# Two of three head groups transposed in 32x32 squares by VectorE and by way of DRAM, in a newly ordered attention pipeline

## Chip, cores and metric

The kernel runs on one core of a Trainium2 chip. The metric is the device time of one execution in microseconds (us); lower is better. All data is fp32.

## What is computed

Thirty-two batches of 256 rows of 384 numbers go through one attention layer with 12 heads of 32 columns. A per-batch matrix `adj` (256 x 256) is added to the scores of every head. Then comes the residual and a layer norm:

```
q = (x @ Wq.T).reshape(B, N, 12, 32)
k = (x @ Wk.T).reshape(B, N, 12, 32)
v = (x @ Wv.T + bv).reshape(B, N, 12, 32)
a = einsum('bnhd,bmhd->bhnm', q, k) * 384**-0.5 + adj[:, None]
a = where(all(a == 0, axis=-1), -inf, a)
a = nan_to_num(softmax(a, axis=-1))
o = einsum('bhnm,bmhd->bnhd', a, v).reshape(B, N, 384)
y = layernorm(x + o @ Wo.T + bo)
```

## The kernel before

The five engines are programmed by hand, each in its own block, and meet through semaphores. Each engine runs a function `step(t)` over the batches (a few steps written out, a loop of two steps per turn, a few more written out). Within an engine the order of the work is the order in which `step` calls its helpers, and nothing else decides it. In step t the kernel *attends* batch t, *finishes* batch t-1 and *projects* batch t+1.

Per batch, the work is this (P = 128 partitions, N = 256 rows in two halves, 12 heads in three groups of four):

- **Projection** (`unit`, helper `product`, L487). K and Q come as three units K01, K2Q0, Q12, V as V0, V1. Each fp32 product is made of three passes over pieces split in high and low parts. ScalarE copies K and Q out of PSUM (`save_kq`, L382), GpSimd splits them (`split_kq`, L292, L294), VectorE adds the bias to V (`save_v`, L746). GpSimd also splits the next x (`split_xt`, L279, L281).
- **Scores** (`scores`, L564), one group at a time, into the four `s_bank`s. VectorE adds `adj`, negates and finds the row's least value in one instruction per head and half (`add_bias`, L724). ScalarE takes the exponential and the row sum (`exps`, L395) into `prob`, a ring of four units. A *unit* is two heads of one half; a batch has 12, units 0 to 3 being group 0, and so on.
- **Transposing**. For the product with V the keys must lie on the partitions. TensorE transposes every unit of `prob` with four matmuls by the identity (`transposes`, L578) into one of two `t_bank`s. VectorE (units 0, 2, 4, 6, 8, 10, L736) and ScalarE (the odd ones, L406) copy the result into `probT`.
- **Weighing** (`weigh`, L615): `probT` times V, 8 matmul pairs per group, into `bank_a`. ScalarE copies it out (`save_o`, L414).
- **Finish**: the reciprocal of the sums (L784) is widened by GpSimd (L312), transposed by TensorE (`spread`, L592), multiplied in (`divide`, L793). ScalarE and GpSimd split the result (L422, L303), TensorE multiplies it by Wo (Y0, Y1), VectorE adds the residual (L803) and takes the moments (L808, L813), GpSimd makes the deviation (`deviation`, L321 to L326), ScalarE normalises (L428). A small matmul (`flag`, L623) looks for rows that are all zero.

The DMAs are all issued by SyncE's queue, in order: per step xt (the transposed x, 384 KB), bias (`adj`, 256 KB), xr (x, 384 KB) and the store of the output (384 KB). PSUM has eight banks: four `s_bank`s, two `t_bank`s, `bank_a` (weighing, spread, K01, flag) and `bank_b` (everything else). In TensorE's step the order is

```
T10 T11 | K2Q0 | weigh 2 | T0 T1 | Q12 | spread | scores 1 | T2 T3 | spread | V0 | weigh 0 | T4 T5
V1 | scores 2 | T6 T7 | K01 | Y0 | T8 T9 | weigh 1 | scores 0 of the next | flag | Y1
```

where T10, T11, weigh 2, spread, Y0 and Y1 belong to batch t-1 and K, Q, V to batch t+1.

Of the kernel before, what the change touches and what calls it, by code (L numbers as in the profile page):

```python
# [3 lines left out]
F32 = mybir.dt.float32  # L4
# [9 lines left out]
P = 128  # L14
# [4 lines left out]
UNITS = H * NT // PAIR  # L19
SCALE = D ** -0.5  # L20
# [5 lines left out]
PT_RING = 2 * JH  # L26
# [4 lines left out]
ON_DVE = (0, 2, 4, 6, 8, 10)  # L31


class Unit:


    def __init__(self, u):
        self.u, self.g, self.c, self.pair = u, u // 4, u // 2 % 2, u % 2
        self.heads = [JH * self.g + PAIR * self.pair + i for i in range(PAIR)]


class Step:


    def __init__(self, i, c):
        self.i, self.c, self.n, self.p = i, c, 2 * i + c, c % 2
        looped = not isinstance(i, int)
        self.attend = looped or 0 <= c < B
        self.finish = looped or 1 <= c <= B
        self.project = looped or -1 <= c <= B - 2  # L50
        self.looped = looped
        self.first = not looped and c == 0
        self.last = not looped and c == B

    def count(self, per_step, extra=0):
        return self.i * (2 * per_step) + (self.c * per_step + extra)

    def before(self):
        return Step(self.i, self.c - 1)

    def after(self):
        return Step(self.i, self.c + 1)

    def slot(self, h):
        return (JH * self.p + h) % PT_RING

    def kq(self, name):

        order = ("K01", "K2Q0", "Q12") if not self.looped and self.c == -1 else ("K2Q0", "Q12", "K01")
        return self.count(3, 3 + order.index(name) + 1)  # L70

    def copies(self, u, on_dve):

        mine = [k for k in range(UNITS) if (k in ON_DVE) == on_dve]
        return self.count(len(mine), len([k for k in mine if k <= u]))

    def unit(self, u):
        return (self, u) if u >= 0 else (self.before(), u + UNITS)


def steps(eng, body):
    for c in range(-1, 3):
        body(Step(0, c))
    with eng.Fori(1, (B - 4) // 2) as i:
        body(Step(i, 1))
        body(Step(i, 2))
    for c in range(B - 3, B + 2):
        body(Step(0, c))


def build(nc, x, xT, adj, wqT, wkT, wvT, bv, woT, bo, out):
# [15 lines left out]
    bias = [sb(f"bias{p}", [P, NT, N]) for p in range(2)]  # L107
    kq = sb("kq", [P, 2 * KC, N])
# [7 lines left out]
    probT = sb("probT", [P, PT_RING, NT, N])  # L116
# [21 lines left out]
    t_bank = [nc.alloc_psum_tensor(f"t_bank{k}", [P, PAIR, NT, P], F32) for k in range(2)]  # L138

    bank_a = nc.alloc_psum_tensor("bank_a", [P, NT * N], F32)  # L140

    bank_b = nc.alloc_psum_tensor("bank_b", [P, NT * N], F32)
# [13 lines left out]
    bias_loaded = [sem(f"bias_loaded{p}") for p in range(2)]  # L156
    xt_hi_ready = sem("xt_hi_ready")
    xt_ready = sem("xt_ready")
    xr_ready = sem("xr_ready")
    kq_done = sem("kq_done")  # L160
    kq_saved = sem("kq_saved")
    kq_hi_ready = sem("kq_hi_ready")
    kq_ready = sem("kq_ready")
# [10 lines left out]
    pv_done = sem("pv_done")  # L174
    o_saved = sem("o_saved")
# [22 lines left out]
    def on_a(t, name):  # L198
        if not t.looped and t.c == -1:
            return name in ("K01", "Q12", "V1")  # L200
        return name == "K01"

    def bank(t, name):
        return bank_a if on_a(t, name) else bank_b

# [3 lines left out]
    with nc.Block() as block:  # L209

        @block.sync
        def _(sp):
            def load_xt(t, k):
                sp.dma_start(xt[(t.c + k) % 2][:], xT[t.n + k].rearrange("(c p) n -> p c n", p=P)
                             ).then_inc(xt_loaded[(t.c + k) % 2], DMA)

            def load_bias(t):
                q = (t.c + 1) % 2
                sp.dma_start(bias[q][:], adj[t.n + 1].rearrange("(c p) m -> p c m", p=P)
                             ).then_inc(bias_loaded[q], DMA)  # L220
# [7 lines left out]
            load_xt(Step(0, 0), 0)  # L228
# [3 lines left out]
            load_bias(Step(0, -1))  # L232
            load_xt(Step(0, 0), 1)
            load_w(W_V, wvT)
            load_b(bv_all, bv)
            load_b(bo_all, bo)
            load_w(W_O, woT)

            def step(t):
                if t.c == -1:  # L240
                    sp.wait_ge(xt_ready, 1)
                    load_xt(t, 3)
                if t.looped or 0 <= t.c <= B - 4:

                    sp.wait_ge(xt_ready, t.count(1, 2))
                    load_xt(t, 3)
                if t.project and (t.looped or t.c >= 0):
                    if t.looped or t.c >= 1:

                        sp.wait_ge(neg_ready, t.count(H * NT))  # L250
                    load_bias(t)
                if t.attend:
                    if t.looped or t.c >= 2:

                        sp.wait_ge(y_saved, t.count(NT, -NT))
                    sp.dma_start(xr[t.p][:], x[t.n].rearrange("(c p) d -> p c d", p=P)
                                 ).then_inc(xr_loaded[t.p], DMA)
                if t.before().finish:
                    sp.wait_ge(y_ready, t.count(NT, -NT))
                    sp.dma_start(out[t.n - 2].rearrange("(c p) d -> p c d", p=P), y_out[:]  # L260
                                 ).then_inc(stored, DMA)
# [5 lines left out]
        def _(pool):  # L267
# [7 lines left out]
            def split_xt(t, k):  # L275
                q = (t.c + k) % 2
                pool.wait_ge(xt_loaded[q], DMA * ((t.c + k) // 2 + 1) + t.i * DMA)
                apart(pool)
                nc.gpsimd.tensor_copy(xt_hi[q][:], xt[q][:]).then_inc(xt_hi_ready, 1)  # L279
                pool.wait_ge(xt_hi_ready, t.count(1, k + 1))  # L280
                nc.gpsimd.tensor_tensor(xt_lo[q][:], xt[q][:], xt_hi[q][:].bitcast(F32), ALU.subtract  # L281
                                        ).then_inc(xt_ready, 1)

            def split_kq(t, name):
                q = (t.c + 1) % 2
                a = KQ_AT[name]
                if t.looped or t.c >= 1:

                    pool.wait_ge(scored, t.count(KC))
                pool.wait_ge(kq_saved, t.kq(name))  # L290
                apart(pool)
                nc.gpsimd.tensor_copy(kq_hi[q][:, a:a + 2, :], kq[:, a:a + 2, :]).then_inc(kq_hi_ready, 1)  # L292
                pool.wait_ge(kq_hi_ready, t.kq(name))
                nc.gpsimd.tensor_tensor(kq_lo[q][:, a:a + 2, :], kq[:, a:a + 2, :],  # L294
                                        kq_hi[q][:, a:a + 2, :].bitcast(F32), ALU.subtract).then_inc(kq_ready, 1)

            def split_o_lo(t):
                if t.looped or t.c >= 2:

                    pool.wait_ge(y_done, t.count(NT, -NT))  # L300
                for k, (a, b) in enumerate(((0, 2), (2, 3))):
                    pool.wait_ge(o_hi_ready, t.count(2, k - 1))
                    nc.gpsimd.tensor_tensor(o_lo[:, a:b], o_n[:, a:b], o_hi[:, a:b].bitcast(F32), ALU.subtract  # L303
                                            ).then_inc(o_ready, 1)

            def widen_inv(t):
                pool.wait_ge(inv_ready, t.count(1))
                if t.looped or t.c >= 2:

                    pool.wait_ge(inv_spread, t.count(2, -2))  # L310
# [4 lines left out]
            def deviation(t):  # L315

                pool.wait_ge(stats_ready, t.count(NT))
                if t.looped or t.c >= 2:
                    pool.wait_ge(y_ready, t.count(NT, -NT))
# [3 lines left out]
                pool.wait_ge(var_ready, t.count(2))  # L323
                nc.gpsimd.tensor_tensor(rstd[:], var_eps[:], halfs[:], ALU.pow).then_inc(pow_ready, 1)
                pool.wait_ge(pow_ready, t.count(1))
                nc.gpsimd.tensor_tensor(shift[:], negmean[:], rstd[:], ALU.mult).then_inc(rstd_ready, 1)  # L326

            def add_bo(t):
                pool.wait_ge(b_loaded, 2 * DMA)
                pool.wait_ge(xr_loaded[t.p], DMA * (t.c // 2 + 1) + t.i * DMA)  # L330
# [3 lines left out]
            def step(t):  # L334
                if t.c == -1:
                    for name in ("K01", "K2Q0", "Q12"):
                        split_kq(t, name)
                    pool.wait_ge(xt_ready, 1)
                    split_xt(t, 2)
                    return  # L340
                if t.finish:
                    widen_inv(t)
                if t.project:
                    split_kq(t, "K2Q0")
                if t.before().finish:
                    deviation(t.before())
                if t.project:
                    split_kq(t, "Q12")
                if t.finish:
                    split_o_lo(t)  # L350
                if t.looped or 0 <= t.c <= B - 3:

                    pool.wait_ge(kq_done, t.count(3, 3))
                    pool.wait_ge(v_done, t.count(2, 2))
                    split_xt(t, 2)
# [543 lines left out]
```

## Time and profile before

| | |
|---|---|
| time, median of 3 runs | 851.68 us (850.9 to 851.9) |
| time of the profiled execution | 852.93 us |
| its span, first to last instruction | 850.9 us |
| TensorE (PE) busy | 826.5 us, 97% |
| ScalarE (ACT) busy | 645.2 us, 76% |
| VectorE (DVE) busy | 557.8 us, 66% |
| GpSimd (POOL) busy | 454.6 us, 53% |
| moved by DMA | 49.30 MB, mean 58 GB/s |
| mean granted TensorE clock | 0.986 |

The profiled execution took 1.25 us more than the median of the runs. Its span leaves out 2.0 us of its own time, which lie before the first and after the last instruction. Matmuls and weight loads are pipelined, so a matmul's own duration is longer than the time it adds. What a group of matmuls costs is read from the chain of waits, which gives each piece of the chain its start, its length and the number of instructions in it.

### The profile page before, as it was taken

How to read it: one execution, taken by the hardware profiler on the slowest of the kernel's cores; microseconds unless marked ns; L12 is line 12 of the kernel's file. 1: busy time of each engine (PE TensorE's matmuls, PEld its weight loads, DVE VectorE, ACT ScalarE, POOL GpSimd, SP SyncE). 2: the span in 40 equal slices, each digit the busy share in tenths (PEclk: the TensorE clock that was granted, in tenths of full speed). 3: DMA queues.
4: the chain of work that ended last, by engine and by line, in shares of the span. 5: the costliest groups of instructions: out<-in, count | busy, mean ns of one | idle time of the engine just before them, and what ended most of it. 6: DMA issues, size and time to landing. Idle time of an engine off the chain costs nothing.

```text
span 850.9 us, 27334 instructions
## 1 busy us (share of the span) xinstructions
PE 826.5 (97%) x8504; PEld 715.3 (84%) x8504; DVE 557.8 (66%) x2152; ACT 645.2 (76%) x2055; POOL 454.6 (53%) x518
## 2 busy tenths in 40 slices
PE   7999999999999999999999999999999999999974
PEld 6888888888888888888888888888888888888853
DVE  3666676766666676667676667676667676667672
ACT  3677787877787877777877777887777787777782
POOL 4455545655545655545655545665454665454522
PEclk8999999999999999999999999999999999999996
DMA  6211221211221111222111222111222110211010
GB/s 198 70 44 40 70 70 52 66 39 47 68 68 55 62 47 39 68 68 66 51 53 33 68 68 68 49 55 31 68 68 68 49 61 25 68 50 51 21 39 37
DMA packets 40864, 49.30 MB, mean 58 GB/s; under 512 B 2176, under 2 KB 40832, under 8 KB 40832
## 3 DMA queue, kind: packets, MB, share of 16 engines
q1 hardware_dynamic: 40832, 48.90, 18.6%
q8 instruction: 17, 0.28, 0.1%
q14 instruction: 15, 0.12, 0.1%
HBM read 36.31 MB, written 12.58 MB: 57 GB/s over the span
## 4 chain that ended last, share of the span: by engine, by line
PE 95%; ACT 1%; DVE 1%; issue 1%; POOL 1%; DMA 1%; SPq 0%; ACTq 0%; POOLq 0%; DVEq 0%
PE bank_b L487 41%; PE t_bank L578 21%; PE bank_a L615 11%; PE s_bank L564 10%; PE bank_a L487 8%; PE bank_a L592 2%; ACT prob L395 1%; DMA w_f<-in_wkT 1%; DVE neg L724 0%; PE bank_a L623 0%; POOL o_lo L303 0%; ACT y_out L428 0%; DVE probT L736 0%; POOL kq_lo L294 0%; DVE y L803 0%
## 5 line engine op out<-in xcount | busy, mean ns | idle before, releaser
L395 ACT ACTIVATE prob<-neg,negmax 128x256 f32<-128x256 f32 x768 | 379.8, 499 | 2.9 <-DVE negmax L724 2.8
L724 DVE CUSTOM_DVE_ANT_0 neg<-s_bank,bias 128x256 f32<-128x256 f32 x768 | 281.0, 419 | 39.0 <-PE s_bank L564 37.7
L578 PE MATMUL t_bank<-ident,prob 128*128 128x128 f32 x1536 | 207.4, 278 | 2.8 <-ACT prob L395 2.8
L578 PEld LDWEIGHTS t_bank<-ident,prob 128*128 128x128 f32 x1536 | 169.0, 140 | 41.3 <-ACT prob L395 18.6
L406 ACT ACTIVATE probT<-t_bank 128x512 f32<-128x512 f32 x192 | 113.4, 591 | 105.5 <-PE t_bank L578 105.5
L312 POOL COPY inv_wide<-inv 128x768 f32<-128x768 f32 x32 | 26.4, 824 | 250.3 <-DVE inv L784 250.3
L395 ACT ACTIVATION_READ_ACCUMULATOR prob<-neg,negmax 128x1 f32 x768 | 146.9, 191 | 0.0
L736 DVE COPY probT<-t_bank 128x512 f32<-128x512 f32 x192 | 131.6, 685 | 1.3 <-PE t_bank L578 1.2
L294 POOL TENSOR_TENSOR kq_lo<-kq,kq_hi 128x512 fp32r<-128x512 f32 x96 | 123.6, 1287 | 7.7
L487 PE MATMUL bank_b<-xt_hi,w_hi 128*128 128x256 f32 x378 | 112.7, 298 | 0.0
L487 PE MATMUL bank_b<-xt_lo,w_hi 128*128 128x256 f32 x378 | 107.0, 283 | 0.0
L487 PE MATMUL bank_b<-xt_hi,w_lo 128*128 128x256 f32 x378 | 107.0, 283 | 0.0
L292 POOL CAST kq_hi<-kq 128x512 fp32r<-128x512 f32 x96 | 58.7, 612 | 87.9 <-ACT kq L382 76.8
L615 PE MATMUL bank_a<-probT,v 128*32 128x256 f32 x1536 | 102.8, 385 | 2.6 <-DVE probT L736 1.8
L803 DVE TENSOR_TENSOR y<-bank_b,xr 128x384 f32<-128x384 f32 x64 | 35.7, 557 | 80.0 <-PE bank_b L487 80.0
L793 DVE TENSOR_TENSOR o_n<-o_raw,bank_a 128x512 f32<-128x512 f32 x64 | 35.1, 549 | 69.1 <-PE bank_a L592 69.1
L303 POOL TENSOR_TENSOR o_lo<-o_n,o_hi 128x512 fp32r<-128x512 f32 x64 | 64.8, 1013 | 23.6 <-ACT o_hi L422 23.6
L487 PEld LDWEIGHTS bank_b<-xt_hi,w_hi 128*128 128x128 f32 x378 | 72.5, 192 | 3.6 <-issue 2.4
L487 PEld LDWEIGHTS bank_b<-xt_lo,w_hi 128*128 128x128 f32 x378 | 72.7, 192 | 0.0
L487 PEld LDWEIGHTS bank_b<-xt_hi,w_lo 128*128 128x128 f32 x378 | 72.4, 192 | 0.0
L487 PE MATMUL bank_b<-w_hi,o_hi 128*128 128x384 f32 x192 | 69.1, 360 | 3.1 <-POOL o_lo L303 2.5
L615 PEld LDWEIGHTS bank_a<-probT,v 128*32 128x32 f32 x1536 | 40.3, 109 | 36.8 <-issue 12.9
(70 smaller groups left out, 1738.6 us busy)
## 6 DMA issues: line engine op xcount, KB each, us to landing
xt<-in_xT SPq DMA_DIRECT2D x32, 384.0 KB, 3.5
xr<-in_x SPq DMA_DIRECT2D x32, 384.0 KB, 3.1
out_y<-y_out SPq DMA_DIRECT2D x32, 384.0 KB, 2.5
bias<-in_adj SPq DMA_DIRECT2D x32, 256.0 KB, 2.7
w_f<-in_wkT SPq DMA_DIRECT2D x3, 192.0 KB, 4.0
w_f<-in_wqT SPq DMA_DIRECT2D x1, 576.0 KB, 6.0
w_f<-in_wvT SPq DMA_DIRECT2D x1, 576.0 KB, 7.8
w_f<-in_woT SPq DMA_DIRECT2D x1, 576.0 KB, 10.2
```

What stands on the lines that cost most here:

```text
L292: nc.gpsimd.tensor_copy(kq_hi[q][:, a:a + 2, :], kq[:, a:a + 2, :]).then_inc(kq_hi_ready, 1)
L294: nc.gpsimd.tensor_tensor(kq_lo[q][:, a:a + 2, :], kq[:, a:a + 2, :], kq_hi[q][:, a:a + 2, :].bitcast(F32), ALU.subtract).then_inc(kq_read ...
L303: nc.gpsimd.tensor_tensor(o_lo[:, a:b], o_n[:, a:b], o_hi[:, a:b].bitcast(F32), ALU.subtract).then_inc(o_ready, 1)
L395: nc.scalar.activation(prob[:, u % PROB_RING, k], neg[:, h, w.c], ACT.Exp, scale=-1.0, bias=negmax[t.p][:, w.c, h:h + 1], accum_out=sums[t ...
L406: nc.scalar.activation(probT[:, a:a + PAIR, :, P * w.c:P * (w.c + 1)], t_bank[u % 2][:], ACT.Copy).then_inc(probT_act, 1)
L487: last = nc.tensor.matmul(ps, w_pair[a](k), m_pair[b](k), start=(k == 0 and e == 0), stop=(k == KC - 1 and e == 2))
L564: last = nc.tensor.matmul(s_bank[j][:, c, :], a[t.p][rows, KC + g, P * c:P * (c + 1)], b[t.p][rows, g, :], start=(e == 0), stop=(e == 2))
L578: last = nc.tensor.transpose(t_bank[u % 2][:, k, m, :], prob[:, u % PROB_RING, k, P * m:P * (m + 1)], ident[:])
L615: last = nc.tensor.matmul(bank_a[HD * j:HD * (j + 1), 0:N], v[t.p][:, m, HD * h:HD * (h + 1)], probT[:, t.slot(h), m, :], start=(m == 0), ...
L724: nc.vector.tensor_tensor_reduce(out=neg[:, h, w.c], in0=s_bank[h % JH][:, w.c, :], in1=bias[t.p][:, w.c, :], scale=-1.0, scalar=BIG, op0= ...
L736: nc.vector.tensor_copy(probT[:, a:a + PAIR, :, P * w.c:P * (w.c + 1)], t_bank[u % 2][:]).then_inc(probT_dve, 1)
L803: nc.vector.tensor_tensor(y[:, c, :], bank(t, f"Y{c}")[:, 0:D], xr[p][:, c, :], ALU.add).then_inc(y_saved, 1)
```

## The change

**Groups 0 and 1 are no longer transposed by TensorE.** For units 0 to 7, VectorE transposes `prob` in squares of 32 x 32 (`square`, new L794 to L805), one instruction per unit, from SBUF to a staging area in SBUF. That area lies over `w_f`, the raw weights, which are no longer needed after their split. The squares then still lie on the wrong partitions. So SyncE stores each group (128 partitions x 8 KB, 1 MB) to a buffer in DRAM and loads it back in another order of rows (`store_squares`, `load_squares`, new L247 to L262), with runs of 2 KB. `weigh` reads the loaded tile in runs of 32 elements. ON_DVE is empty: the copies of the four units that TensorE still transposes (8 to 11) are all ScalarE's.

**Keys in a row.** For the load to have whole runs, keys 4r+b of a half are put in place 32b+r: `save_kq` writes K01 in that order, and groups 0 and 1 take `adj` from a second copy, `adjP`, with its columns in the same order (made once on the host, outside the device's time). This adds one DMA of 256 KB per step (`bias_sq`). Group 2 reads the first `adj` against scores whose K2 lies in the old order.

**Banks.** The two `t_bank`s become one (`bank_t`), and the bank so freed is `bank_c` (K01 and spread). `bank_a` keeps the weighing and the flag, `bank_b` the rest.

**Orders and stages.** The order of every engine is new. In step t, TensorE attends batch t from its scores 2 on, projects K01 and V0 of batch t+1 and makes its scores 0 and 1, projects K2Q0 and Q12 of batch t+2, weighs groups 1 and 2 of batch t-1 and multiplies batch t-2 by Wo. There are separate semaphores for the three K and Q units and for the three groups of the weighing.

```diff
-PT_RING = 2 * JH
-ON_DVE = (0, 2, 4, 6, 8, 10)
+SQ = 32
+BLOCKS = P // SQ
+SQUARED = 2
+TURNED = SQUARED * GROUP
+ON_PE = tuple(range(TURNED, UNITS))
+ON_DVE = ()
...
+    bias_sq = [sb(f"bias_sq{p}", [P, NT, N]) for p in range(2)]
+    probT = sb("probT", [P, H - SQUARED * JH, NT, N])
+    sq_probT = [sb(f"sq_probT{g}", [P, BLOCKS, JH, NT, NT, SQ]) for g in range(SQUARED)]
+    AREA = BLOCKS * JH * NT * NT * SQ
+    w_space = w_f[:].rearrange("p w c n -> p (w c n)")
+    sq_dram = [nc.dram_tensor(f"sq_dram{g}", (P, BLOCKS, AREA // BLOCKS), F32, kind="Internal").ap()
+               for g in range(SQUARED)]
...
-    t_bank = [nc.alloc_psum_tensor(f"t_bank{k}", [P, PAIR, NT, P], F32) for k in range(2)]
+    bank_t = nc.alloc_psum_tensor("bank_t", [P, PAIR, NT, P], F32)
...
+            def store_squares(t, g):
+                sp.wait_ge(squared, t.count(TURNED, GROUP * (g + 1)))
+                after(sp, sq_loaded[g], t.count(DMA))
+                sp.dma_start(sq_dram[g], sq_stage[g].rearrange("p b h m c s -> p b (h m c s)")
+                             ).then_inc(sq_stored[g], DMA)
+            def load_squares(t, g):
+                sp.wait_ge(sq_stored[g], t.count(DMA, DMA))
+                after(sp, pv_done[g], t.count(1))
+                sp.dma_start(sq_probT[g][:].rearrange("p i h m c s -> p i (h m c s)"),
+                             sq_dram[g].rearrange("(i r) b n -> (r b) i n", i=BLOCKS)).then_inc(sq_loaded[g], DMA)
...
 # SyncE's step
+                if t.alive:
+                    store_squares(t, 0)
+                    load_squares(t, 0)
+                    store_squares(t, 1)
+                    load_xr(t)
+                    load_squares(t, 1)
+                if nxt2.alive and not nxt2.first:
+                    load_bias_sq(nxt2)
+                if prev2.alive:
+                    store_out(prev2)
...
+            def square(t, u):
+                w = Unit(u)
+                dve.wait_ge(prob_ready, t.count(H * NT, PAIR * (u + 1)))
+                if u % GROUP == 0:
+                    after(dve, sq_stored[w.g], t.count(DMA))
+                a = w.heads[0] % JH
+                nc.vector.transpose(sq_stage[w.g][:, :, a:a + PAIR, :, w.c].rearrange("p b h m s -> p (h m) b s"),
+                                    prob[:, u % PROB_RING].rearrange("p k (m b r) -> p (k m) b r", m=NT, b=BLOCKS)
+                                    ).then_inc(squared, 1)
...
 # TensorE's weigh
+                if g < SQUARED:
+                    pe.wait_ge(sq_loaded[g], t.count(DMA, DMA))
...
+                        if g < SQUARED:
+                            weights = sq_probT[g][:, :, j, m].rearrange("p i c s -> p c i s")
+                        else:
+                            weights = probT[:, h - SQUARED * JH, m, :]
```

TensorE's new order of a step (names as above; -1 and -2 are the batches before, +1 and +2 those after):

```
T11(-1) | V1 | K01(+1) | Y0(-2) | weigh 1(-1) | scores 2 | K2Q0(+2) | weigh 2(-1) | T8 | Y1(-2)
spread(-1) | flag | T9 | scores 0(+1) | Q12(+2) | weigh 0 | T10 | spread(-1) | V0(+1) | scores 1(+1)
```

How instructions move, at three places. First TensorE in the middle of a step. Before, between Q12 (`bank_b`) and V0, two units of transposes stand back to back (eight matmuls) behind the scores (`s_bank`):

```order
L592 MATMUL bank_a<-ident,inv_wide 128x128 x4
L564 MATMUL s_bank<-kq_hi 128x256 x4
L564 MATMUL s_bank<-kq_lo,kq_hi 128x256 x4
L564 MATMUL s_bank<-kq_hi,kq_lo 128x256 x4
L564 MATMUL s_bank<-kq_hi 128x256 x4
L564 MATMUL s_bank<-kq_lo,kq_hi 128x256 x4
L564 MATMUL s_bank<-kq_hi,kq_lo 128x256 x4
L578 MATMUL t_bank<-ident,prob 128x128 x8
```

Now, from the last product of Q12 on, with `sq_probT` the tile that came back from DRAM:

```order
L539 MATMUL bank_b<-xt_hi,w_lo 128x256
L626 MATMUL bank_a<-sq_probT,v 32x256 x8
L596 MATMUL bank_t<-ident,prob 128x128 x4
L607 MATMUL bank_c<-ident,inv_wide 128x128 x2
L539 MATMUL bank_b<-w_hi,xt_hi 128x384
```

Only single units of four transposes are left, and each stands between other work.

Second, VectorE. Before, between `add_bias` of units 9 and 10 (each head an instruction and its read of the accumulator), a copy out of PSUM:

```order
L724 ISA neg,negmax<-s_bank,bias 128x256
L724 ISA negmax 128x1
L736 COPY probT<-t_bank 128x4x128
L724 ISA neg,negmax<-s_bank,bias 128x256
L724 ISA negmax 128x1
```

Now, behind unit 3's `add_bias` at the beginning of a step (`w_f` is the staging area):

```order
L789 ISA neg,negmax<-s_bank,bias_sq 128x256
L789 ISA negmax 128x1
L803 STREAM_TRANSPOSE w_f<-prob 128x4x4x32
L823 TENSOR_TENSOR v<-bank_b,bv_all 128x384
L803 STREAM_TRANSPOSE w_f<-prob 128x4x4x32
```

Six copies a step are gone and eight square transposes are in.

Third, SyncE's queue with its waits. Before, a step:

```order
L214 DMA xt<-in_xT 128x3x256 [waits xt_ready]
L219 DMA bias<-in_adj 128x2x256 [waits neg_ready]
L256 DMA xr<-in_x 128x2x384 [waits y_saved]
L260 DMA out_y<-y_out 128x2x384 [waits y_ready]
```

Now a step, from the second half of the loop:

```order
L252 DMA sq_dram<-w_f 128x2048 [waits squared,sq_loaded0]
L256 REGISTER_ALU
L261 DMA sq_probT<-sq_dram 128x4x512 [waits sq_stored0,pv_done0]
L248 REGISTER_ALU
L252 DMA sq_dram<-w_f 128x2048 [waits squared,sq_loaded1]
L245 ISA [waits y_saved]
L245 DMA xr<-in_x 128x2x384
L261 DMA sq_probT<-sq_dram 128x4x512 [waits sq_stored1,pv_done1]
```

Four DMAs of 1 MB per step are new, and each load waits in the queue for its own store to have landed.

## Rows read from the trace of the kernel before

**Rows 1.** The profile's page, section 1: busy time of each engine over the span

```profile
PE 826.5 (97%) x8504; PEld 715.3 (84%) x8504; DVE 557.8 (66%) x2152; ACT 645.2 (76%) x2055; POOL 454.6 (53%) x518
```

**Rows 2.** Busy by stretch, two whole steps inside the loop

```profile
core 0: us, PE busy (x) PEld busy (x) DVE busy (x) ACT busy (x) POOL busy (x), PEclk, DMA share, GB/s
300.11:350.92 50.81, 50.81 (x531) 44.15 (x531) 34.36 (x135) 39.91 (x128) 28.44 (x32) 1.00 0.18 57
```

**Rows 3.** Chain of waits inside the loop: start us, us, what

```profile
299.24 0.87 PE t_bank L578 x8
...
304.49 2.16 PE bank_b L487 x18
306.65 0.44 PE bank_a L592 x4
307.08 0.91 PE s_bank L564 x24
308.00 1.02 PE t_bank L578 x8
309.02 0.22 PE bank_a L592 x2
309.24 1.59 PE bank_b L487 x9
310.83 1.00 PE bank_a L615 x16
...
322.88 0.12 PE bank_a L623
```

**Rows 4.** The same chain, where steps 1, 2 and 30 begin

```profile
45.20 1.11 PE t_bank L578 x8
...
70.68 0.87 PE t_bank L578 x8
...
781.86 0.87 PE t_bank L578 x8
```

**Rows 5.** VectorE's timeline: start us, us, line, tiles, shapes, count

```profile
300.53 0.69 DVE L736 COPY probT<-t_bank 128x512 f32<-128x512 f32 x1
301.13 0.41 DVE L724 CUSTOM_DVE_ANT_0 neg<-s_bank,bias 128x256 f32<-128x256 f32 x1
301.47 0.42 DVE L724 CUSTOM_DVE_ANT_0 neg<-s_bank,bias 128x256 f32<-128x256 f32 x1
```

**Rows 6.** Groups by form: count, busy us, mean ns of one, idle before

```profile
L395 ACT ACTIVATE prob<-neg,negmax 128x256 f32<-128x256 f32 x768 | 379.8, 499 | 2.9 <-DVE negmax L724 2.8
L406 ACT ACTIVATE probT<-t_bank 128x512 f32<-128x512 f32 x192 | 113.4, 591 | 105.5 <-PE t_bank L578 105.5
L281 POOL TENSOR_TENSOR xt_lo<-xt,xt_hi 128x768 fp32r<-128x768 f32 x31 | 57.4, 1851 | 2.5
```

**Rows 7.** DMA issues: KB each, median us from issue to landing

```profile
xr<-in_x SPq DMA_DIRECT2D x32, 384.0 KB, 3.1
out_y<-y_out SPq DMA_DIRECT2D x32, 384.0 KB, 2.5
bias<-in_adj SPq DMA_DIRECT2D x32, 256.0 KB, 2.7
```

**Rows 8.** Busy by stretch while the first loads run

```profile
4.00:10.00 6.00, 4.69 (x26) 3.71 (x25) 3.13 (x6) 2.73 (x4) 0.00 (x0) 0.86 1.01 335
8.00:14.00 6.00, 5.78 (x35) 5.78 (x36) 1.53 (x2) 2.15 (x3) 1.90 (x2) 0.72 1.05 300
```

**Rows 9.** Chain of waits, the end of the last batch

```profile
824.43 0.66 PE t_bank L578 x4
...
836.22 3.23 PE bank_b L487 x9
...
840.09 3.26 PE bank_b L487 x9
```

More of the change, by code:

```diff
@@ L61, in after, with count @@
[L61 to L70, printed above, removed]
+        self.looped = not isinstance(i, int)
+        self.alive = self.looped or 0 <= c < B
+        self.first = not self.looped and c == 0
+    def count(self, per_batch, extra=0):
+        return self.i * (2 * per_batch) + (self.c * per_batch + extra)
@@ L239, in step @@
             def step(t):
[L240 to L261, printed above, removed]
+                nxt2 = t.later(2)
+                nxt = t.later(1)
+                prev2 = t.later(-2)
+                if nxt2.alive and (nxt2.looped or nxt2.c >= 2):
+                    load_xt(nxt2)
+                if nxt.alive and not nxt.first:
+                    load_bias(nxt)
+                if t.alive:
[8 more added lines that the diff above has]
+                    store_out(prev2)
             steps(sp, step)
@@ L334, in step @@
             def step(t):
[L335 to L355, printed above, removed]
-                if t.attend:
+                nxt2 = t.later(2)
+                nxt = t.later(1)
+                prev = t.later(-1)
+                prev2 = t.later(-2)
+                if prev.alive:
+                    widen_inv(prev)
+                if nxt2.alive and not nxt2.first:
+                    split_xt(nxt2)
+                if nxt.alive:
+                    split_kq(nxt, "K2Q0")
+                    split_kq(nxt, "Q12")
+                    split_kq(nxt, "K01")
+                if prev2.alive:
+                    deviation(prev2)
+                if t.alive:
                     add_bo(t)
-                if t.project:
-                    split_kq(t, "K01")
+                if prev.alive:
+                    split_o_lo(prev, 0)
+                    split_o_lo(prev, 1)
             steps(pool, step)
@@ L635, in step @@
             def step(t):
-                if t.c == -1:
-                    for name in ("K01", "K2Q0", "Q12"):
-                        unit(t, name)
-                    scores(t.after(), 0)
-                    return
-                if t.first:
-                    unit(t.before(), "V0")
-                    unit(t.before(), "V1")
-                if t.finish:
-                    transposes(t.before(), 10)
-                    transposes(t.before(), 11)
-                if t.project:
-                    unit(t, "K2Q0")
```

717 lines of the change are left out of this document (368 added, 349 removed).

## Prediction

> **What bounds the kernel now.** I read the page's busy shares first [rows 1]: TensorE is busy for 97% of the span, ScalarE for 76, VectorE for 66. Such shares are means over stages, so I took the busy table of two steps inside the loop next [rows 2]: there TensorE is busy for 50.81 of 50.81 us at the full granted clock (1.00, the 2.4 GHz level), ScalarE for 39.91, VectorE for 34.36, GpSimd for 28.44, and the DMA engines for 0.18 of the time. So a step takes 25.4 us and TensorE alone sets it. The chain of waits says the same: in the loop it holds TensorE pieces only, and these lengths are what each piece adds [rows 3]. A K or Q unit costs 2.16, a V or Y unit 1.59, a weighing 1.00, scores of a group 0.91, the two spreads 0.44 and 0.22, the flag 0.12, and two units of transposes 0.87 or 1.02. Six such pairs stand in a step, two at 0.87 and four at 1.02, 5.8 us together. Check: 3 x 2.16 + 4 x 1.59 + 3.0 + 2.73 + 0.66 + 0.12 + 5.8 = 25.2, the 25.4 of the table but for 0.2. Steps begin at 45.20 (step 1), 70.68 (step 2) and 781.86 (step 30) [rows 4]: 28 steps in 711.2 us. The rest of the 850.9 us is 70.7 of head and 69.0 of tail.
>
> **TensorE.** Eight of twelve units leave. The four left stand alone between other work. A pair costs 0.15 more behind weighing or scores than behind a projection (1.02 against 0.87), so a unit alone is not half a pair: its lower end is 0.51, its upper one the 0.66 of a lone unit in the tail [rows 9]. I take 0.55, nearer the loop's row, since the tail's unit had just waited: 2.2 us a step in place of 5.8. The step becomes 25.4 - 3.6 = 21.8 us. The weighings of groups 0 and 1 read their tile in runs of 32; no row shows such a read. I keep 1.00 each, because the tile is as large and the runs are long, with 1.5 as upper end (1 us a step).
>
> **VectorE.** Two steps hold 34.36 us of its work, 17.2 in one. Six copies go. A copy of 512 elements starts 0.60 before the next instruction (300.53 to 301.13) [rows 5], so 13.6 us stay. What a square transpose of 512 elements takes is not in this trace. Lower end: half the elements' time; 256 elements in `add_bias` cost 0.34 from start to start [rows 5], 0.26 less than 512, so 0.34. Upper end: two ticks per element, 0.60 + 2 x 0.26 = 1.12. I take 0.60, the row with the same number of elements. 13.6 + 8 x 0.60 = 18.4 of 21.8 us. The Trainium skill, Vector Engine (DVE) Microarchitecture Reference, section on the reshape front-end, has the transposing array sustain one element per cycle and lane, which would be my 0.60; no run so far shows it.
>
> **ScalarE.** 19.96 us a step, less two copies of 0.59 at most [rows 6] and 0.5 in fact, since such durations overlap: 19.0 of 21.8. K01's copy now writes with a stride; at double its cost it adds 0.6, and 2 us of cover are left. Its 24 exponentials (499 ns and the accumulator's read) are untouched.
>
> **The DMAs.** A step moves 1.44 MB now (three times 384 KB and 256 KB). Added are 4 x 1.05 MB and 0.26: 5.9 MB. The rate: 57 GB/s at a share of 0.18 [rows 2] is 317 GB/s for a full share, and in the first loads full rings moved 335 and 300 [rows 8]. So 18.6 us of transfers a step (17.6 to 19.7): busy, but under 21.8. The round trip: 128 KB more cost 0.4 us (256 KB in 2.7, 384 in 3.1) [rows 7]; by that rate and the 317, a load of 1 MB takes 3.1 + 2.1 = 5.2 us and a store, from the 2.5 of the output's, 4.6.
>
> **Do the waits fit?** I laid one step along TensorE's new order, with 0 at T11. V1 ends at 2.1, K01 at 4.3, Y0 5.9, weigh 1 at 6.9, scores 2 at 7.8, K2Q0 at 10.0, weigh 2 at 11.0, Y1 13.1, scores 0 of the next 15.2, Q12 17.3, weigh 0 18.3, V0 20.7, scores 1 21.7. VectorE has unit 3's square (the fourth) behind it at 4.4: store at 9.0, load landed at 14.2, weigh 0 wants it at 17.3. 3 us to spare. Unit 7's square ends near 9.8. Its store queues behind that load, lands at 17.3, and the load goes out then: landed near 23.5, which is 1.7 of the next step, wanted at 5.9. 4 us to spare. The tightest places are others: scores 1 needs VectorE's unit 3 (0.5 us to spare); the second spread needs the first `divide` (0.8); K2Q0 of t+2 needs its x loaded and split. That x is issued behind the output's store, which waits in SyncE's queue for ScalarE's last `normalise` at 20.2. It then queues in the rings behind the 1 MB load, lands near 4 of the next step, takes 2.8 in GpSimd (1.85 of it the subtraction [rows 6]) and is wanted at 7.8, 1 us to spare. GpSimd's widening and splits fill the time up to 12.5, scores 0 wants them at 14.3. So no wait ends last in my table. Misses of 0.1 to 0.3 in single rows are covered, of 1 us not: 0 to 1 us of stall a step is the range, 0 my value.
>
> **Ends.** Head: the first Q unit has to wait for its weights as before, steps 0 and 1 miss parts. By the same table scores 1 of batch 0 end near 26 us; step 0 is ScalarE's (16), step 1 TensorE's without Y (21.8 - 3.2): 61 where the kernel before has 70.7. Tail: step 30 lacks two projections, and ScalarE then bounds it (18); from step 31 on I count 45 (T11, Y0, the last weighings, Y1, and then the last batch's finish with its two Y units at 3.2 each at the lower clock [rows 9]): 63 against 69.
>
> **Sum.** 61 + 28 x 21.8 + 63 = 734 us of span, plus the 2.0 outside it: **736 us**, against 852.9 of the profiled execution. The median of the runs was 1.25 lower than that execution; I leave this out.
>
> **Rivals.**
> 1. *VectorE becomes the bound.* A square takes 1.12 us: 13.6 + 9.0 = 22.6, and in its order it waits about 1 us more for Y0 and for scores: 23.6 a step, 736 + 28 x 1.8 = 786 us. For it: no row prices the square. Against it: the copy's row, with as many elements. Chance 0.13.
> 2. *The rings become the bound.* They idle where SyncE waits for a store to land before it issues the load, about 1.7 us for group 0 and 0.5 for group 1. With 5.9 MB the step is 5.9 MB / rate + 2.2: 20.8 us at 317 GB/s, 23.3 at 280. That gives 736 + 28 x 1.5 = 778 us. For it: half of the new bytes are written to DRAM at once before they are read, and 300 was the rate of one full stretch [rows 8]. Against it: longer runs (2 KB) than any in this trace. The Trainium skill, DMA: Bandwidth & Descriptors, section on latency, gives HBM access as 0.2 us on average and 2 us at high load. No row here shows the latter. An estimate by that page: each transfer takes 1.8 longer, the two gaps grow by 3.6, the step is 24.4 and the whole 809 us. Chance of this rival 0.17.
> 3. *Slower than before: the round trip through DRAM at a low rate.* The same loop of store, wait and load in SyncE's queue decides from 250 GB/s down: 23.6 + 2.2 = 25.8 a step, and 736 + 28 x 4.0 = 848. At 235 GB/s it is 27.3, 890 us. For it: stores and loads of 1 MB to and from one DRAM buffer are new. Against it: the 317 of the loop and the quick landing of the output's store. Chance 0.07.
>
> That the edit does not do what it says I rule out: the instruction order shows 4 of 12 units left on TensorE.
>
> **Numbers.** Forecast 0.62, its own range 722 to 757 (a unit of transposes at 0.51; 0.7 us of stall). The rest, 0.01, is a result near no change. A measurement of this kernel can tell 0.2% from none. The range must reach into rivals 1 and 2 and hold four fifths: 720 to 795. Faster 0.91, same 0.01, slower 0.08.
>
> **What would show it.** Steps of 21.8 us in the loop's busy table, with TensorE at over 20.8 of them. Square transposes near 0.60 from start to start. Landing of the 1 MB load near 5.2 and of the store near 4.6, a DMA share near 0.85. If the chain of waits holds VectorE's squares, rival 1 is right; if weigh 0 or the x split wait for a DMA, rival 2 or 3. A granted clock under 1.00 in the loop would mean stalls I left out, and a weighing piece over 1.00 for groups 0 and 1 a cost I set to nothing.

## Result, and the profile after

The changed kernel takes 881.47 us (median of 4 runs, 879.22 to 883.38), the kernel before 851.75 (850.9 to 851.9). The ratio is 1.035, with a 95% interval of 1.032 to 1.038. The forecast was 736.0 us, its range 720 to 795. The kernel is slower, and by none of the three rivals.

The page of the profile after: busy times, the granted clock and the DMA share in 40 slices, the queues, the chain by engine, some groups and the DMA issues (KB each, us to landing).

```profile
PE 748.5 (85%) x7480; PEld 636.9 (72%) x7480; DVE 597.4 (68%) x2216; ACT 618.7 (70%) x1991; POOL 452.1 (51%) x518
...
PEclk8989999899798988979899797998979989899965
DMA  7277787577374774747667375774747747477740
...
q14 instruction: 76, 0.62, 0.2%
...
PE 75%; issue 12%; DMA 4%; DVE 3%; POOL 2%; ACT 2%; SPq 0%; DVEq 0%; ACTq 0%; POOLq 0%
...
L803 DVE STREAM_TRANSPOSE w_f<-prob 128x512 f32<-128x512 f32 x256 | 173.1, 695 | 2.9 <-issue 2.8
...
sq_dram<-w_f SPq DMA_DIRECT2D x64, 1024.0 KB, 5.5
sq_probT<-sq_dram SPq DMA_DIRECT2D x64, 1024.0 KB, 5.7
```

The same two rows of the page before, which have no notches and few packets:

```profile
PEclk8999999999999999999999999999999999999996
...
q14 instruction: 15, 0.12, 0.1%
```

Against the page before [rows 1], TensorE's busy time fell from 826.5 to 748.5 us, as it was meant to, but its share fell from 97% to 85%: it waits. The granted clock is notched, which it was not before, and so is the DMA share. The chain holds 12% of "issue", time in which an engine waits for nothing that the profile shows.

Busy by stretch in the changed kernel: the second row runs free, the first and the third take in a notch (the columns are those of [rows 2]).

```profile
327.50:355.00 27.50, 24.57 (x241) 21.30 (x245) 19.65 (x75) 17.88 (x58) 12.16 (x14) 0.85 0.48 171
450.00:480.00 30.00, 30.00 (x324) 25.61 (x326) 24.33 (x97) 25.24 (x84) 17.46 (x20) 1.00 0.79 280
500.00:554.00 54.00, 46.53 (x467) 40.12 (x466) 36.82 (x138) 38.32 (x124) 28.60 (x33) 0.91 0.62 222
```

Between notches the kernel does what the prediction said: TensorE is busy for all of 30.00 us at clock 1.00 (the 2.4 GHz level), with the rings at a share of 0.79. The chain of waits shows what a notch is (start us, length us, what):

```profile
428.85 0.23 PE bank_c L607 x2
...
429.31 0.06 DVEq L85
429.36 5.11 issue
...
434.84 0.42 DVE neg L789
435.27 0.34 DVE neg L789
435.61 2.29 issue
437.90 0.09 DVE negmax L789
438.04 1.65 PE s_bank L585 x21
...
454.36 0.54 PE bank_t L596 x4
...
482.11 5.20 issue
```

L85 is the line `with eng.Fori(2, 15) as i:` in `steps`, so `DVEq L85` is the loop's own work, with which VectorE goes from the end of a turn back to the top. There VectorE does nothing for 5.11 us, runs the first instructions of unit 3's `add_bias`, and does nothing for another 2.29. The same comes at 482.11, one turn (two steps) later. The waits of VectorE and what hangs on them (us in all, times, the longest):

```profile
ACT prob L444 <- DVE negmax L789: 141.0, 55, 9.0
...
PE s_bank L585 <- DVE negmax L789: 91.8, 13, 7.9
DVE neg L789 <- issue: 63.8, 12, 5.7
...
DVE negmax L789 <- issue: 27.4, 12, 2.3
```

Twelve times each: the loop has 13 turns, so 12 branches back. And queue 14 of kind "instruction" carried 76 packets where the kernel before has 15. The stretch from 420 to 474 us, about one turn, holds five of them, while the kernel before has a single one between 180 and 760 us. Two of the five start within the first pause and one within the second (the queue's row for 429.3 to 434.5 us, then for 435.6 to 437.95):

```profile
q14 instruction: 2, 0.02, 0.8%
...
q14 instruction: 1, 0.01, 0.9%
```

From one `reciprocal` to the next VectorE takes 31.3 and 22.0 us in turn. Steps of 22.0 are near the forecast; those that hold the branch back are 9.3 us longer.

### The profile page after: what moved, and what is told of

It is laid out like the page before. It is cut to its first block, busy times and chain, and to the rows that moved or that the text cites. A ratio compares the mean times of both kernels' runs of the same rounds, so it can differ in the third digit from the quotient of the medians.

```text
span 881.1 us, 25233 instructions
## 1 busy us (share of the span) xinstructions
PE 748.5 (85%) x7480; PEld 636.9 (72%) x7480; DVE 597.4 (68%) x2216; ACT 618.7 (70%) x1991; POOL 452.1 (51%) x518
## 4 chain that ended last, share of the span: by engine, by line
PE 75%; issue 12%; DMA 4%; DVE 3%; POOL 2%; ACT 2%; SPq 0%; DVEq 0%; ACTq 0%; POOLq 0%
PE bank_b L539 38%; PE bank_a L626 10%; PE s_bank L585 10%; PE bank_t L596 8%; PE bank_c L539 7%; PE bank_c L607 2%; DVE neg L789 2%; DMA xt<-in_xT 2%; DMA sq_dram<-w_f 1%; POOL o_lo L351 1%; DMA w_f<-in_wqT 1%; DMA xr<-in_x 1%; ACT prob L444 1%; POOL xt_lo L330 0%; DVE w_f L803 0%
## 5 line engine op out<-in xcount | busy, mean ns | idle before, releaser
L789 DVE CUSTOM_DVE_ANT_0 neg<-s_bank,bias_sq 128x256 f32<-128x256 f32 x512 | 191.4, 411 | 111.5 <-issue 63.8
L803 DVE STREAM_TRANSPOSE w_f<-prob 128x512 f32<-128x512 f32 x256 | 173.1, 695 | 2.9 <-issue 2.8
L585 PE MATMUL s_bank<-kq_hi 32*128 32x256 f32 x768 | 69.0, 349 | 93.0 <-DVE negmax L789 91.8
L585 PEld LDWEIGHTS s_bank<-kq_hi 32*128 32x128 f32 x768 | 39.9, 198 | 120.2 <-DVE negmax L789 100.7
L789 DVE CUSTOM_DVE_ANT_0 neg<-s_bank,bias 128x256 f32<-128x256 f32 x256 | 92.3, 416 | 12.3 <-ACT prob L444 10.5
L596 PE MATMUL bank_t<-ident,prob 128*128 128x128 f32 x512 | 89.5, 301 | 0.7 <-ACT probT L454 0.7
L596 PEld LDWEIGHTS bank_t<-ident,prob 128*128 128x128 f32 x512 | 57.7, 149 | 34.4 <-issue 29.4
L789 DVE DVE_READ_ACCUMULATOR2_ANT negmax<- 128x1 f32 x768 | 63.6, 83 | 27.4 <-issue 27.4
L539 PE MATMUL bank_b<-w_hi,xt_hi 128*128 128x384 f32 x192 | 76.1, 396 | 0.7 <-ACT kq L427 0.7
L454 ACT ACTIVATE probT<-bank_t 128x512 f32<-128x512 f32 x128 | 74.9, 585 | 1.1 <-PE bank_t L596 1.0
```

The lines of the kernel that those rows point to most:

```text
L454: nc.scalar.activation(probT[:, a:a + PAIR, :, P * w.c:P * (w.c + 1)], bank_t[:], ACT.Copy).then_inc(probT_act, 1)
L539: last = nc.tensor.matmul(ps, w_pair[a](k), m_pair[b](k), start=(k == 0 and e == 0), stop=(k == KC - 1 and e == 2))
L585: last = nc.tensor.matmul(s_bank[j][:, c, :], a[t.p][rows, KC + g, P * c:P * (c + 1)], b[t.p][rows, g, :], start=(e == 0), stop=(e == 2))
L596: last = nc.tensor.transpose(bank_t[:, k, m, :], prob[:, u % PROB_RING, k, P * m:P * (m + 1)], ident[:])
L789: nc.vector.tensor_tensor_reduce(out=neg[:, h, w.c], in0=s_bank[h % JH][:, w.c, :], in1=by[t.p][:, w.c, :], scale=-1.0, scalar=BIG, op0=AL ...
L803: nc.vector.transpose(sq_stage[w.g][:, :, a:a + PAIR, :, w.c].rearrange("p b h m s -> p (h m) b s"), prob[:, u % PROB_RING].rearrange("p k ...
```

## Experiments

The theory after this reading: VectorE's loop lies in its program so that the instructions at its top are no longer at hand when it branches back, and they come again by DMA. The Trainium skill, Runtime: NRT & Kernel Launch, section on instruction fetch mechanics, describes this: an engine's instruction memory holds 512 instructions and is refilled in blocks of 256, and "a taken branch whose target isn't in the current 2-page window forces a DMA fetch". The packets inside the two pauses agree with that; the size of the blocks is tested below. The rivals were a stall by the rings' load, and a wait on something that the profile does not name, which the new order of the steps would bring.

**VectorE's steps written out, without a loop.**

```diff
+def flat_steps(eng, body):
+    for c in range(-2, 34):
+        body(Batch(0, c))
...
-            steps(dve, step)
+            flat_steps(dve, step)
```

> Edit: VectorE's 36 steps are written out; the other engines keep their loop. Theory A (VectorE's branch back at the end of each turn makes it fetch its instructions again: 9.2 us from 428.9 to 438.0 in the changed kernel's chain, 13 turns, about 117 us): no such stretch is left, the loop's steps are 21.8 us each, the time falls to 760 to 775 us. Rival B (the pipeline's order itself or the busy DMA rings cost it and the branch only happens to stand there): the idle time moves to another wait and the time stays within 15 us of 881.

Measured: 767.13 us (766.03 to 768.3), ratio to the kernel before 0.9015 (0.8999 to 0.903). The notches are gone (two rows of its page):

```profile
PEclk8999999999999999999999999999999999999975
...
q14 instruction: 38, 0.30, 0.1%
```

Every VectorE instruction with an effect is the same, so the 114 us belonged to the branch back.

**Only the loop's place moved.** Instructions that are never executed (in the branch for a zero in the flag, which no batch takes) ahead of the loop: 4 times N of them, with N = 4, 8, 24 and 32. The traces of these four runs and of the changed kernel all hold 25233 instructions, so none of the added ones ran.

```diff
                 with dve.If_ne(any_zero, 0):
+                    if not t.looped and t.c < 4:
+                        for _ in range(N):
+                            apart(dve)
```

N = 8, 32 instructions:

> Edit: 8 more instructions in each of the four untaken branches ahead of VectorE's loop, 32 in all, never executed; the loop itself is the same but lies 32 instructions further on. Theory A with place (the loop of 277 instructions lies over four blocks of 128 instructions, and fits in three when moved): the fetches in the loop and the stall go, 760 to 780 us. Theory A without place (every branch back costs a fetch): still 880. Rival B: 880.

Measured: 769.94 us (767.91 to 770.7), ratio 0.9039 (0.9021 to 0.9056), 18 instruction packets on queue 14. Thirty-two instructions that nobody runs took 111 us off.

N = 4, 16 instructions:

> Edit: 4 instructions in each of the four untaken branches, 16 in all, half of what pad8 had. If the place of the loop decides by crossing a boundary between blocks of 128 instructions, the effect is all or nothing: 770 us (the loop is then within three blocks) or 881 us (still four); a value between would speak against blocks. I expect 770 with a chance of 0.7.

Measured: 766.76 us (766.52 to 769.8), ratio 0.9017 (0.8996 to 0.9037). N = 32, 128 instructions:

> The changed kernel with 4 times 32 = 128 VectorE instructions ahead of its loop, in branches that are never taken; nothing else differs. The runs so far moved the loop by 16 and by 32 instructions, and both took the loss away (766.8 and 769.9 us). That leaves open how coarse the pieces are in which VectorE gets its instructions. Theory A: the pieces that decide are of 128 instructions. Then a shift of exactly 128 puts the loop back in the same place within its pieces as in the changed kernel: 875 to 885 us, successive steps 31.3 and 22.0 us in turn, some 75 instruction packets on VectorE's queue. Theory B: they are of 256 instructions. Then a loop of 277 instructions shifted by 128 touches two pieces and not three: 765 to 771 us, steps 21.7 to 22.3 us, some 20 packets. Theory C: any 16 or more instructions help, whatever their number, because only the entry or the target of the branch matters: as B, so that a result of 770 tells A from the others alone.

Measured: 881.8 us (880.54 to 883.76), ratio 1.0358 (1.034 to 1.0376): theory A, pieces of 128 instructions. The rows of its page and of its waits are those of the changed kernel again:

```profile
q14 instruction: 78, 0.63, 0.2%
```

```profile
DVE neg L789 <- issue: 62.3, 12, 5.5
```

N = 24, 96 instructions:

> The changed kernel with 4 times 24 = 96 never-taken VectorE instructions ahead of its loop. So far: shifts of 0 and 128 lose 112 us, shifts of 16 and 32 lose nothing, and the loop of the kernel before (269 instructions, starting at the 304th of its program) loses nothing there, but 7.1 us a turn once it starts at the 451st. Theory A: VectorE gets its instructions in pieces of 128, keeps four, and fetches one ahead; a loop of 277 stalls only where it touches four pieces, which is so for 20 starts of 128 (and for 12 with 269). From the five places above, those 20 starts end at most 15 places behind the start of the changed kernel, so a shift by 96 lies clear of them: 765 to 771 us, steps 21.7 to 22.3, some 20 instruction packets on VectorE's queue. Theory B: a wider part of the 128 places is bad, and 16 and 32 were lucky: 875 to 885 us and some 75 packets.

Measured: 772.76 us (771.67 to 773.85), 17 packets, steps 21.7 to 22.4 in the loop but for its first turn: theory A again, but 1.8 us above the range given. In the first turn one interval takes 27.8 us (23.1 with N = 4), and it makes most of the difference. The chain has a wait of 7.30 us for an x transfer in it, and 0.27 us at the branch back, so it is no stall of this kind.

So what decides comes again after 128 instructions: shifts of 0 and 128 lose, 16, 32 and 96 don't. A shift of 64 was not run, so these times alone don't exclude a period of 64; the size of the packets speaks for 128. A packet of queue 14 has 8.2 KB (0.62 MB by 76). By the 32 KiB for 512 instructions of the Trainium skill, Runtime: NRT & Kernel Launch, section on instruction fetch mechanics, that is 128 instructions, an estimate. The blocks of 256 instructions that the same section of the Trainium skill states would have made the shift by 128 a fast kernel, and the measurement decides against that size here.

**The kernel before, with its loop moved** by 3 x 49 = 147 such instructions, from the 304th to the 451st place of the program (the changed kernel's loop starts at the 447th):

```diff
                 with dve.If_ne(any_zero, 0):
+                    if not t.looped and t.c < 4:
+                        for _ in range(49):
+                            apart(dve)
```

> Edit: the kernel before, with 49 more instructions in each of the three untaken branches ahead of VectorE's loop, which moves it to where the changed kernel's loop lies. Theory A with place: instruction packets now appear inside the loop and each turn gets a stall; with the rings nearly idle I expect 2 to 6 us a turn of which VectorE's spare time in this kernel covers a part: 865 to 910 us. Rival B and theory A without place: 852, no change.

Measured: 937.69 us (937.47 to 938.79), ratio 1.102 (1.1002 to 1.1038). First its page and its waits, then its chain at one branch back (L84 is the line of the `with` here):

```profile
q14 instruction: 76, 0.62, 0.2%
```

```profile
DVE y L806 <- issue: 83.6, 12, 7.1
```

```profile
376.63 0.06 DVEq L84
376.68 3.34 issue
380.02 0.05 DVEq L84
380.07 2.30 issue
```

That the move brings the stall was expected, its price was not: 2 to 6 us a turn and at most 910 us stood in the expectation, and the time is 28 us above. Nothing of the change is in this kernel, and it has the same 12 stalls and 76 packets. Its turns take 57.96 us against 50.82: 7.1 us each, 86 in all. The stall needs neither the squares nor full rings.

**How much the full rings add.** The squares' transfers carry a quarter of their bytes and leave the rest out, once with VectorE's loop and once written out (the loaded tiles are cleared at the start, which is cut here):

```diff
-                sp.dma_start(sq_dram[g], sq_stage[g].rearrange("p b h m c s -> p b (h m c s)")
+                sp.dma_start(sq_dram[g][:, :, 0:128], sq_stage[g].rearrange("p b h m c s -> p b (h m c s)")[:, :, 0:128]
...
-                             sq_dram[g].rearrange("(i r) b n -> (r b) i n", i=BLOCKS)).then_inc(sq_loaded[g], DMA)
+                             sq_dram[g].rearrange("(i r) b n -> (r b) i n", i=BLOCKS)[:, :, 0:128]).then_inc(sq_loaded[g], DMA)
```

> Edit: each of the four 1 MB transfers moves a quarter of its bytes (256 KB), with the same number of runs; the tile is cleared once at the start. It leaves out three quarters of the squares' transport, so its output isn't the reference's. Theory A, stall made of the fetch alone: the stall at the turn stays near 9 us and the time falls by less than 10 us. Theory A, stall made long by full rings: it shrinks to 3 or 4 us a turn, 790 to 815 us. Rival B with the rings as the bound: below 780 us, with no stall at the turn.

> Edit: VectorE written out, and the squares' transfers move a quarter of their bytes. It leaves out three quarters of the squares' transport. Theory C in its wide form (head and tail are long because the transfers of 1 MB stand in them): 740 to 752 us. Rival (they are long for other reasons, the order in which the pipeline fills): 760 to 767.

Measured: 849.15 us (845.43 to 852.45) with the loop, 757.48 (756.32 to 758.74) written out, ratios 0.9965 and 0.8898. Both lie between the times that were expected: with the loop the time fell by 32 us, neither by less than 10 nor to 815 and below, and the stall became 7.7 us a turn and not 3 or 4; written out, it is above 752 and below 760. The rows for the first one, its VectorE waits and landings:

```profile
DVE negmax L791 <- issue: 34.5, 12, 3.2
...
DVE neg L791 <- issue: 9.2, 4, 3.2
```

```profile
sq_dram<-w_f SPq DMA_DIRECT2D x64, 256.0 KB, 2.6
sq_probT<-sq_dram SPq DMA_DIRECT2D x64, 256.0 KB, 3.1
```

Per turn 51.35 - 43.69 = 7.7 us are lost with quiet rings, 53.46 - 43.95 = 9.5 with full ones (the changed kernel against N = 4). So full rings add about 2 us a turn. In the stretch of the first pause above (429.3 to 434.5 us) the DMA engines are full with the squares' and other transfers; that the instruction packets wait behind these fits, but no run shows it by itself. With VectorE written out in both, a step in the loop of the other engines takes 21.85 us with a quarter of the bytes and 22.1 on average with all. So inside the loop the transports cost 0.2 us a step on average, most of it in a few steps of up to 23.0.

**All engines written out, and x loaded earlier.**

> Edit: all five engines written out, no loop at all. Theory A (only VectorE's loop overflowed): as with VectorE's alone, 767 us within 3. Rival (the loops of ScalarE or the queue cost something too): 762 or less, or more if TensorE's longer program makes it wait for fetches.

Measured: 782.14 us (779.42 to 787.25), 15 more than with VectorE alone written out. A queue row of its page, and a row of its waits:

```profile
q8 instruction: 61, 1.00, 0.5%
```

```profile
PEld bank_b L544 <- issue: 26.2, 19, 4.9
```

Queue 8 has 61 packets of 16 KB where the changed kernel has 15, and TensorE's weight loads of `bank_b` wait 26.2 us for "issue", in 19 places, against 13.0 in 5 with VectorE alone written out. So straight code has a price on TensorE, whose loop did fit. It need not be all of the 15 us: three other engines were written out as well, queue 14 has 60 packets against 38, and GpSimd's waits for the transposed x rose from 24.3 to 36.8 us. No run divides the sum. In this kernel x was then loaded right behind the load of group 0's squares:

```diff
-                if nxt2.alive and (nxt2.looped or nxt2.c >= 2):
-                    load_xt(nxt2)
...
+                if nxt3.alive and nxt3.c >= 2:
+                    load_xt(nxt3)
```

> Edit to all_flat: SyncE issues the next x load right behind the load of group 0's squares, a batch earlier, instead of behind the output's store. Theory C (what is left of my miss, 767 against 736, is in good part transfers that are issued late: the x load stands in the chain for about 5% of the span): head shorter by 4 to 8 us and the steps of 22.0 to 22.3 become 21.8: 752 to 760 us. Rival (the miss is elsewhere): 766 within 2.

Measured: 779.97 us (776.49 to 784.59): not to be told from the one before. The wait moved, it did not go: GpSimd waits 9.9 us in all for the transposed x, but 100.0 for the residual's, where it was 20.3:

```profile
POOL xr L384 <- DMA xr<-in_x: 100.0, 32, 10.9
```

**The same idea on the looped kernel with N = 4**: x for the step three ahead behind the load of group 1's squares, and then also GpSimd's addition of the output bias behind its last split, in the last step (what the diff leaves out are the first steps' loads, and that SyncE's loop is a turn shorter for them).

```diff
+                if not early and nxt3.alive:
+                    load_xt(nxt3)
...
-                if t.alive:
+                last = not t.looped and t.c == B - 1
+                if t.alive and not last:
```

> The changed kernel with the 16 never-taken instructions that gave 766.8 us, and with one thing moved on SyncE: x of the step three ahead is now loaded right behind the load of group 1's squares, where it stood behind the output store of the step, which waits for the output. In the run with 16 instructions the chain of waits has the x transfer in it, and GpSimd's split of x waits for it. If the rings' order is what costs the last 0.2 us of a step (22.0 against 21.8) and some of the long steps at the start, the time is 759 to 764 us. If the x transfer is only pushed from one place to another, so that the residual's x or the output waits in its stead, as it did when x was moved further forward in the kernel that is written out for every engine, it is 765 to 770.

> The kernel of the run before this one, with GpSimd's addition of the output bias in the last step put behind the split of the last output operand, which TensorE waits for at the end (the prediction took 1 to 2 us for this order in the tail). If that addition is on the path at the end, the time is 1 to 2 us below the run before this one, so 758 to 763; if the residual's x, which arrives late there, sets the end, no difference that can be measured. Beside both: the time of the kernel before is 851.7, so the ratio should be 0.89 to 0.90.

Measured: 766.61 us (764.46 to 768.21) and 765.5 (763.12 to 768.08, 5 runs), ratio of the last 0.8981 (0.8959 to 0.9002). Against 766.76 for N = 4 alone neither gains anything that can be told apart. In the last step the transfer on the chain changed from the residual's x (5.86 us) to the round trip of group 0's squares (3.86 and 6.21), and the end came no sooner. What stands is one result: the change with a few idle instructions ahead of its loop is 10% faster than the kernel before.

## Why the prediction was wrong

**The step that failed is "Do the waits fit?".** It laid one step along TensorE's order and let every engine pass from a step's end to the next one's top for nothing. "So no wait ends last in my table" is true of semaphores and DMAs; the table had no line for the branch back at L85, and so none for the instructions that VectorE needs behind it. The stated range for stalls of 0 to 1 us a step missed 9.5 us a turn, 4.8 a step. The runs showed in its place a pause of VectorE at every branch back, for instructions that come again by DMA. Nothing in the trace before pointed to it, since its loop of 269 instructions at the 304th place stalls nowhere. But the instruction order of the changed kernel shows the loop at the 447th place with 277. It was the move, not the eight more instructions: 269 at the 451st stall too.

The accounting, from the starts of steps 2 and 30 in the chains. In the changed kernel:

```profile
75.88 0.59 PE bank_t L596 x4
...
805.38 0.59 PE bank_t L596 x4
```

In the kernel with N = 4:

```profile
75.17 0.59 PE bank_t L596 x4
...
691.03 0.59 PE bank_t L596 x4
```

28 steps take 729.5 us in the changed kernel and 615.9 with N = 4; the forecast was 28 x 21.8 = 610.4. So of the miss of 147 us in the profiled span (881.1 against 734), 113.6 are the stalls (12 x 9.5), 5.5 steps of 22.0 for 21.8, 14.9 the head and 12.7 the tail.

Point by point, the rest:

- **TensorE's step: right.** The lone units add 0.48 to 0.59 in the chain, against 0.55; a weighing of a squared tile 1.00, against 1.00; both as written. A clear step is 21.8 to 22.0. Within it two errors cancel in part: the two K, Q units that stand behind scores cost 2.35 each, not 2.16 (0.4 a step too little), and the flag adds 0.01, not 0.12. In the kernel before, K2Q0 costs 2.35 and 2.26 in two steps (chain at 300.11 and 325.56), which is why the sum of pieces came out 0.2 short of the 25.4.
- **VectorE: right.** A square takes 0.63 from start to start, against 0.60 for the copy of as many elements. The Trainium skill, Vector Engine (DVE) Microarchitecture Reference, section on the reshape front-end, has the array sustain one element per cycle and lane. The 0.63 agrees with it, and is far from the 1.12 of two ticks per element. The timeline (start us, length us, operation) in the changed kernel:

```profile
461.14 0.71 DVE L803 STREAM_TRANSPOSE w_f<-prob 128x512 f32<-128x512 f32 x1
461.77 0.52 DVE L823 TENSOR_TENSOR v<-bank_b,bv_all 128x384 f32<-128x384 f32 x1
```

  Two clear steps of the kernel with N = 4, 298.7 to 342.6 us, hold 36.34 us of VectorE's work, 18.2 a step against 18.4, and 38.05 of ScalarE's, 19.0 against 19.0:

```profile
298.70:342.60 43.90, 43.78 (x468) 37.40 (x468) 36.34 (x139) 38.05 (x125) 28.35 (x32) 1.00 0.75 266
```

- **ScalarE's strided copy: right.** "At double its cost": 1103 ns for K01 against 598 for the two other pairs.
- **The DMAs: nearly.** Store 5.5 us against 4.6, load 5.7 against 5.2, share 0.75 against 0.85, since full rings moved more than 317 GB/s (266 at 0.75 is 355). Rival 2's wait in SyncE's queue does not set the step: a quarter of the bytes gains 0.2 us.
- **Rival 1** fell with the 0.63, **rival 3** with the 355 GB/s. That the kernel was slower is not to rival 3's credit.
- **The sign in "What would show it"** was right: a granted clock under 1.00 in the loop did mean stalls left out. TensorE's 7480 matmuls were busy for 748.5 us with the stalls and 719.5 without, 29 us or 2.4 a turn. The two pauses in the chain are 5.11 + 2.29 = 7.4 a turn; with this 2.4 that is 9.8, near the 9.5.
- **Head: mis-sized.** 75.2 with N = 4 against 61. With a quarter of the bytes it is still 71.3, so 4 us are transfers (4.58 and 8.49 for two stores and 7.46 for an x queued behind them, in the chain with N = 4) and 10 are orders of work. "Step 0 is ScalarE's" and "step 1 TensorE's" failed. In the quarter kernel without the loop VectorE is busy for 11.60 of the 12.00 us from 30 to 42, in step 0, and ScalarE for 8.91; step 1 begins at 48.03 where I had 42. The scores 0 that TensorE makes in step 1 for the next batch wait for GpSimd, which has two splits of x and three K, Q units to do in a row with nothing done ahead:

```profile
55.97 1.84 POOL xt_lo L335
...
58.45 1.29 POOL kq_lo L346
...
60.38 1.28 POOL kq_lo L346
...
62.29 1.28 POOL kq_lo L346
63.61 0.98 PE s_bank L590 x22
```

- **Tail: mis-sized.** 73.7 with N = 4 against 63 (and 69.0 before). Step 30 took 21.2 where I had 18, and the last part 52.5 where I had 45; with a quarter of the bytes the tail is still 72.3. The last batch's chain goes through ScalarE, VectorE and GpSimd in turn, and I had counted engines, not that chain. No run took it apart further.

## What to carry to other kernels

A loop on an engine has a place as well as a length. Before trusting a forecast for a rolled loop, compare its instruction count and start with a version known to run clean, and look in the profile for instruction packets inside the loop and for "issue" behind the branch back. If they are there, shift the loop by a few idle instructions or write out that one engine; here these two came out alike (766.76 and 767.13 us), while writing out all engines cost 15 us more. A hand-laid table of steps must be carried through the first and the last steps too, engine by engine, since buffers that are filled ahead inside the loop are not yet so there.

## What the runs showed that was not expected

- The same VectorE work takes 881 or 767 us by the place of its loop alone, and a shift by 128 instructions brings the loss back. The places (stalls at shifts 0 and 128, and for the kernel before at the 451st; none at 16, 32, 96, and none at the 304th) agree with pieces of 128, of which four are held and one more is fetched ahead, so that a loop that touches four stalls and one that touches three does not. Five packets a turn agree with it too. That count of held pieces was inferred, not shown by a run of its own.
- The price is per branch back: 7.1 us (kernel before, rings at 53 GB/s), 7.7 (quarter of the bytes), 9.5 (full rings).
- TensorE's granted clock pays again for another engine's stall. In the 2 us behind the pause, with TensorE idle from 431 to 438 us, it is 0.50 (the 1.2 GHz level), and from 443 us on it is 1.00 again:

```profile
438.00:440.00 2.00, 1.96 (x26) 1.74 (x27) 1.78 (x4) 0.00 (x0) 0.00 (x0) 0.50 0.02 4
...
443.00:446.00 3.00, 3.00 (x24) 3.00 (x24) 2.48 (x11) 3.00 (x10) 2.10 (x3) 1.00 0.11 44
```

  The scores behind the pause add 1.65 us in the chain, where those of the kernel with N = 4 add 0.98.
- Even where the loop's place is good, steps alternate between 21.7 and 22.2 us, and those of 22.2 hold the branch back. A turn of 43.95 us is 0.25 above two steps of 21.85.
